# Maximum over the partitions: block transposes and small copies on VectorE instead of transposes on TensorE

## What is computed

```python
xn = _layernorm(x, axis=-1)
q = xn @ wq.T + bq;  k = xn @ wk.T + bk;  v = xn @ wv.T + bv
scores = jnp.einsum('bqd,bkd->bqk', q, k) * 256 ** -0.5
attn = softmax(scores, axis=-1) @ v
lilora = up_aux @ (lora_up @ (lora_down @ down_aux))
out = x + attn + (xn @ W.T + b) + xn @ lilora.T
```

## Time and profile before

| | |
|---|---|
| median of 3 runs | 580.87 us (580.44 to 581.39) |
| the profiled execution, its own time | 580.21 us |
| its span | 578.3 us |
| mean granted TensorE clock | 0.985 of full speed |
| TensorE busy (weight loads) | 549.9 us, 95% (518.6 us, 90%) |
| VectorE busy | 370.9 us, 64% |
| ScalarE busy | 308.9 us, 53% |
| GpSimd busy | 249.7 us, 43% |

### The profile page before, as it was taken

The page is one execution under the profiler, slowest core; times in us unless marked ns, Lnnn a source line. Parts: engine busy times, 40 slices in busy tenths (PEclk is TensorE's granted clock), DMA queues, the critical chain, the costliest instruction groups (busy, mean ns, idle before and its releaser), DMA issues.

```text
span 578.3 us, 10296 instructions
## 1 busy us (share of the span) xinstructions
PE 549.9 (95%) x3958; PEld 518.6 (90%) x3958; DVE 370.9 (64%) x873; ACT 308.9 (53%) x753; POOL 249.7 (43%) x149
## 2 busy tenths in 40 slices
PE   3898999999999999999999999999999999999995
PEld 2687999998999899999999989999999999999994
DVE  3555776666786576757766667866767576666671
ACT  3565346655565456573466655554565744544452
POOL 2801563454514663325634445146633256333333
PEclk9699899999999999999999999999999999999998
DMA  7100000011000300002000120002000000000001
GB/s 247 57 18 1 0 19 19 20 39 73 18 2 19 92 19 20 19 1 92 19 20 19 31 80 19 2 20 91 19 19 20 1 20 19 19 19 19 19 19 37
DMA packets 9300, 18.90 MB, mean 33 GB/s; under 512 B 2240, under 2 KB 3876, under 8 KB 8356
## 3 DMA queue, kind: packets, MB, share of 16 engines
q1 hardware_dynamic: 7712, 18.09, 9.0%
q10 hardware_dynamic: 1540, 0.16, 0.2%
HBM read 9.86 MB, written 8.39 MB: 32 GB/s over the span
## 4 chain that ended last, share of the span: by engine, by line
PE 79%; ACT 8%; DMA 6%; DVE 5%; issue 1%; POOL 1%; SPq 0%; ACTq 0%; POOLq 0%
PE s_ps L677 9%; PE s_ps L679 9%; PE o_ps L770 9%; PE s_ps L678 9%; PE o_ps L774 9%; PE o_ps L772 9%; PE g_ps L677 6%; PE g_ps L678 6%; PE g_ps L679 6%; DMA x_sb<-in_L_attn_x 5%; ACT s L426 4%; ACT p_hi L434 2%; PE g_ps L697 2%; PE g_ps L751 1%; DVE s L578 1%
## 5 line engine op out<-in xcount | busy, mean ns | idle before, releaser
L341 POOL TENSOR_TENSOR p_lo<-s,p_hi 128x1024 fp32r<-128x1024 f32 x64 | 153.8, 2404 | 307.1 <-ACT p_hi L434 196.8
L770 PE MATMUL o_ps<-v_hi,p_hi 128*128 128x258 f32 x512 | 149.8, 293 | 3.8 <-POOL p_lo L341 3.8
L677 PE MATMUL s_ps<-xt_hi,zt_hi 128*128 128x256 f32 x512 | 146.7, 287 | 0.0
L679 PE MATMUL s_ps<-xt_hi,zt_lo 128*128 128x256 f32 x512 | 145.4, 284 | 0.0
L678 PE MATMUL s_ps<-xt_lo,zt_hi 128*128 128x256 f32 x512 | 145.3, 284 | 0.0
L774 PE MATMUL o_ps<-v_hi,p_lo 128*128 128x258 f32 x512 | 144.8, 283 | 0.0
L772 PE MATMUL o_ps<-v_lo,p_hi 128*128 128x256 f32 x512 | 144.7, 283 | 0.0
L426 ACT ACTIVATE s<-s,e 128x256 f32<-128x256 f32 x256 | 109.3, 498 | 27.4 <-DVE s L578 27.4
L562 DVE SCALAR_TENSOR_TENSOR tile_max<-s_ps,e,tile_max 128x256 f32<-128x256 f32 x224 | 108.3, 484 | 23.4 <-PE s_ps L679 13.4
L770 PEld LDWEIGHTS o_ps<-v_hi,p_hi 128*128 128x128 f32 x512 | 96.9, 189 | 5.7 <-issue 3.9
L677 PEld LDWEIGHTS s_ps<-xt_hi,zt_hi 128*128 128x128 f32 x512 | 98.4, 192 | 1.9
(11 more groups left out here) (117 smaller groups left out, 739.4 us busy)
## 6 DMA issues: line engine op xcount, KB each, us to landing
out<-base SPq DMA_DIRECT2D x31, 256.0 KB, 2.5
x_sb<-in_L_attn_x SPq DMA_DIRECT2D x7, 1024.0 KB, 5.7
x_sb<-in_L_attn_x SPq DMA_DIRECT2D x4, 256.0 KB, 5.2
s<-in_L_attn_wk SPq DMA_DIRECT2D x1, 256.0 KB, 6.5
s<-in_L_attn_wq SPq DMA_DIRECT2D x1, 256.0 KB, 7.3
s<-in_L_attn_wv SPq DMA_DIRECT2D x1, 256.0 KB, 7.3
s<-in_L_ffn_W SPq DMA_DIRECT2D x1, 256.0 KB, 7.5
out<-base SPq DMA_DIRECT2D x2, 128.0 KB, 1.9
```

The source lines that it names most:

```text
L341: nc.gpsimd.tensor_tensor(p_lo[g % 2][:, keys, :], s[:, keys, :], p_hi[g % 2][:, keys, :].bitcast(f32), ALU.subtract)\
L677: nc.tensor.matmul(ps, left_hi(d), right_hi(d), start=(d == 0), stop=False)
L679: mm = nc.tensor.matmul(ps, left_lo(d), right_hi(d), start=False, stop=(d == DT - 1))
L770: nc.tensor.matmul(o_ps[u][:, 0:D + ONES], p_hi[g % 2][:, n, q], v_hi[i][:, n, :], start=(n == 0), stop=False)
```

## The change

The maximum over the partitions is made by VectorE alone, in a new `make_top`:

1. a 32x32 block transpose of `tile_max` into `tile_max_t` (each 32x32 block by itself): within each quadrant of 32 partitions the queries of a block now lie on the partitions;
2. a reduction over the 32 columns of each of the 8 blocks into `quad_max`, which leaves, in each of the four quadrants, the maxima over that quadrant's keys;
3. three copies that gather the other quadrants' results (32 x 8) beside those of the first;
4. a reduction over the four, into `max_col` (32 x 8);
5. three copies that spread it to the other quadrants;
6. a block transpose of `max_col` spread over 32 columns, into `top`.

All ten instructions are linked by semaphores where one needs the other. TensorE's `transpose_max` and `broadcast_max` are gone, and with them the waits of groups for the banks of the maximum; all groups now wait for the group two before them only. ScalarE's `make_top` is gone. In VectorE's loop the order changes too: `make_top`, `make_group_lo` of the second group and the four shifts come right behind the last `make_tile_max`, then `make_out`, then the statistics.

```diff
+            def make_top(g):
+
+                wait(dve, shifted, SB * g)
+                dve.wait_ge(tile_max_made, TILES * (g + 1))
+                nc.vector.transpose(tile_max_t[:, :], tile_max[:, :]).then_inc(max_t_made, 1)
+                dve.wait_ge(max_t_made, g + 1)
+                nc.vector.tensor_reduce(quad_max[:, 0, :], tile_max_t[:, :].rearrange("p (j k) -> p j k", k=BLOCK),
+                                        AXIS, ALU.max).then_inc(block_max_made, 1)
+                dve.wait_ge(block_max_made, g + 1)
+                for r in range(1, QUADS):
+                    nc.vector.tensor_copy(quad_max[0:BLOCK, r, :], quad_max[r * BLOCK:(r + 1) * BLOCK, 0, :])\
+                      .then_inc(quads_gathered, 1)
+                dve.wait_ge(quads_gathered, (QUADS - 1) * (g + 1))
+                nc.vector.tensor_reduce(max_col[0:BLOCK, :], quad_max[0:BLOCK, :, :].rearrange("p r j -> p j r"),
                                         AXIS, ALU.max).then_inc(max_col_made, 1)
+                dve.wait_ge(max_col_made, g + 1)
+                for r in range(1, QUADS):
+                    nc.vector.tensor_copy(max_col[r * BLOCK:(r + 1) * BLOCK, :], max_col[0:BLOCK, :])\
+                      .then_inc(quads_spread, 1)
+                dve.wait_ge(quads_spread, (QUADS - 1) * (g + 1))
+                nc.vector.transpose(top[:, :], max_col[:, :].unsqueeze(2).to_broadcast([PT, Q // BLOCK, BLOCK]))\
+                  .then_inc(top_made, 1)
...
@@ VectorE, start-up
-            make_group_lo(0, 2 * NT)
-            make_group_lo(0, 2 * NT + 1)
-            make_max_col(0)
-            make_group_lo(0, 2 * NT + 2)
-            make_group_lo(0, 2 * NT + 3)
+            make_top(0)
+            for n in range(4):
+                make_group_lo(0, 2 * NT + n)
...
@@ VectorE, loop
+                    if ahead:
+                        make_top(g + 1)
+                    if more:
+                        make_group_lo(b + 1, PLACES * c + 1)
+                    if ahead:
+                        for j in range(SB):
+                            shift(g + 1, j)
+                    make_out(b, c * QT)
                     if b + 2 < B and c < 3:
                         if c == 0:
                             dve.wait_ge(x_loaded[b % 2], DMA * ((b + 3) // 2))
                         make_stats(b + 2, [range(0, 2), range(2, 5), range(5, TILES)][c])
-                    if more:
-                        make_group_lo(b + 1, PLACES * c + 1)
-                    if ahead:
-                        make_max_col(g + 1)
                     if b + 2 < B and c == 2:
                         make_mean_var(b + 2)
-                    make_out(b, c * QT)
-                    if ahead:
-                        for j in range(SB):
-                            shift(g + 1, j)
...
@@ TensorE, a group's wait for its bank
-                if b > 0 and k % PLACES < 2:
+                if b > 0:
                     pe.wait_ge(group_done, max(NG * b + k - 1, NG))
-                elif b > 0 and k % PLACES == 2:
-                    pe.wait_ge(max_col_made, CHUNKS * (b - 1) + k // PLACES + 2)
-                elif b > 0:
-                    pe.wait_ge(top_made, CHUNKS * (b - 1) + k // PLACES + 2)
...
@@ TensorE, in p_times_v and the loop
-                    if u == 0 and n == TILES // 2 and ahead:
-                        transpose_max(g + 1)
...
-                        if u == 0 and ahead:
-                            broadcast_max(g + 1)
...
@@ ScalarE, loop
-                        make_top(g + 1)
```

More of the change, by code:

```diff
@@ L44, in attention_plus_lora_ffn @@
     ONES = 2
+    BLOCK = 32
+    QUADS = PT // BLOCK
     RANK, DDIM = lora_down.shape
@@ L120, in attention_plus_lora_ffn @@
         top = sb("top", [PT, Q])
-        max_col = sb("max_col", [PT, QT])
+        tile_max_t = sb("tile_max_t", [PT, Q])
+        quad_max = sb("quad_max", [PT, QUADS, Q // BLOCK])
+        max_col = sb("max_col", [PT, Q // BLOCK])
         s = sb("s", [PT, TILES, Q])
@@ L202, in attention_plus_lora_ffn @@
         tile_max_made = sem("tile_max_made")
-        max_t_mm = sem("max_t_mm")
+        max_t_made = sem("max_t_made")
+        block_max_made = sem("block_max_made")
+        quads_gathered = sem("quads_gathered")
         max_col_made = sem("max_col_made")
-        top_mm = sem("top_mm")
+        quads_spread = sem("quads_spread")
         top_made = sem("top_made")
@@ L240, in attention_plus_lora_ffn @@
         PLACES = NG // CHUNKS
[L242 to L246, removed]
         block = ctx.enter_context(nc.Block())
@@ L414, in make_e @@
                 nc.scalar.activation(e[b % 2][:, :], e_sum[:, :], ACT.Identity, bias=e_const).then_inc(e_made, 1)
[L416 to L420, removed]
             def make_p(g, j):
@@ L465, in _ @@
                 make_group_hi(0, 2 * NT + n)
-            make_top(0)
             for n in range(4, TILES):
@@ L555, in make_tile_max @@
                         dve.wait_ge(e_made, b + 1)
-                        wait(dve, max_t_mm, g)
+                        wait(dve, max_t_made, g)
                         nc.vector.tensor_scalar(tile_max[:, :], scores, e[b % 2][:, 0:1], None, ALU.add)\
@@ L563, in make_tile_max @@
                                                        ALU.add, ALU.max).then_inc(tile_max_made, 1)
[L565 to L569, removed]
-                                        AXIS, ALU.max).then_inc(max_col_made, 1)
+            def make_top(g):
[11 more added lines that the diff above has]
+                nc.vector.tensor_reduce(max_col[0:BLOCK, :], quad_max[0:BLOCK, :, :].rearrange("p r j -> p j r"),
+                                        AXIS, ALU.max).then_inc(max_col_made, 1)
+                dve.wait_ge(max_col_made, g + 1)
[5 more added lines that the diff above has]
+                  .then_inc(top_made, 1)
             def shift(g, j):
@@ L729, in scores, with p_times_v @@
                 mm.then_inc(score_mm, 1)
-            def transpose_max(g):
-                if g > 0 and (g - 1) // CHUNKS + 1 < B:
-                    pe.wait_ge(group_done, NG * ((g - 1) // CHUNKS + 1) + PLACES * ((g - 1) % CHUNKS) + 1)
-                else:
-                    wait(pe, max_col_made, g)
-                pe.wait_ge(tile_max_made, TILES * (g + 1))
-                for u in range(QT):
-                    mm = nc.tensor.transpose(max_bank(g)[:, u * PT:(u + 1) * PT], tile_max[:, u * PT:(u + 1) * PT],
-                                             identity[:, :])
-                mm.then_inc(max_t_mm, 1)
-            def broadcast_max(g):
-                if g > 0 and (g - 1) // CHUNKS + 1 < B:
-                    pe.wait_ge(group_done, NG * ((g - 1) // CHUNKS + 1) + PLACES * ((g - 1) % CHUNKS) + 2)
-                else:
-                    wait(pe, top_made, g)
-                pe.wait_ge(max_col_made, g + 1)
-                for u in range(QT):
-                    mm = nc.tensor.transpose(top_bank(g)[:, u * PT:(u + 1) * PT],
-                                             max_col[:, u:u + 1].to_broadcast([PT, PT]), identity[:, :])
-                mm.then_inc(top_mm, 1)
-            def p_times_v(g, u, ahead):
+            def p_times_v(g, u):
                 b, c = divmod(g, CHUNKS)
@@ L859, in _ @@
                     for u in range(QT):
-                        p_times_v(g, u, ahead)
-                        if u == 0 and ahead:
-                            broadcast_max(g + 1)
+                        p_times_v(g, u)
                         if more:
```

4 lines of the change are left out of this document (removed).

## The result

The changed kernel takes **561.19 us** (median of 4 runs, 560.42 to 561.81), beside 580.65 us for the kernel before on the same chip (4 runs, 579.35 to 581.39): a ratio of 0.967, with 95% from 0.9645 to 0.9688. Forecast were 560.0 us, in a range of 558.5 to 564.0. Its profiled execution took 560.91 us, with a span of 559.1 us (before 580.21 and 578.3) at a mean granted clock of 0.984 (before 0.985).

A forecast was written before the change was run, and what follows sets the result against it. TensorE was taken to bound the kernel (busy 66.25 of 67.50 us a batch). 12.9 + 7.4 + 0.5 + 0 = 20.8 us off 580.21 gives 559.4, so a median of 560.0 us, range 558.5 to 564.0.

The forecast's parts named there:

- The transposes: TensorE's stream: removing the transposes saves 0.43 us a block, over 30 blocks 12.9 us.
- The five waits: TensorE's waits ahead of L751 for max_col, behind statistics waiting for x: all go by the new order, 7.4 us.
- make_top: VectorE's new maximum over the partitions: 2.3 us, with 1.8 from below and 3.5 from above.
- twice three copies (0.08 + 0.08 + 0.19 = 0.35): In make_top on VectorE: each set of three small copies takes 0.35 us, 0.7 us for both sets.
- The ends: Kernel's two ends: last tile_max to first shift of block 31, 2.78 us before, gains 0.5 us; the start-up costs 0.
- The start: Start-up, tile_max to shifts on VectorE: make_top and four group_lo pairs fit, done at 47.7, cost 0.
- Room up to a top of 3.2: VectorE's spare time inside the batches: make_top may last up to 3.2 us at no cost there; 0.9 us to spare.
- A: Rival: make_top longer than 3.2 us but the scheme works; 565 us at 3.5, mostly 562 to 566; 12%.
- D: Rival: slower; make_top's ten steps cost 0.51 us each, 5.1 us, 584.4 us; slower than before from 4.8 us; 3%.
- B: Rival: the wait for x only moves and TensorE meets it at group 4; 7.4 us lost, 567.4 us; 7%.
- C: Rival: TensorE's transposes were hidden and removing them gives nothing; 572.9 us; 3%.
- copies would be held by 0.2 us: Block c = 0 of a batch: GpSimd's products hold VectorE's copies 0.2 us, taken in by the 0.9 us to spare.

The follow-up runs named there:

- transposes back: Changed kernel with two unused pairs of 128x128 transposes per block put back into TensorE's stream: 572.97 us, ratio 0.9868.
- statistics back: Changed kernel with the statistics of batch b+2 again ahead of make_top: 576.91 us, ratio 0.9935.
- p_hi first: Changed kernel with, in the last block, all products with p_hi made first and those with p_lo last: 556.67 us, ratio 0.9606.
- tile_max ahead: Changed kernel with tile_max of the first two banks ahead of the last group's lo part and of make_out: 561.73 us, ratio 0.9679.

## Why the prediction came out

The forecast was 1.2 us too low. Its two large terms were right and for the reasons given; two small ones were mis-sized, and the room it gave make_top was wrong in kind, which by luck didn't show.

1. **The transposes: right.** 12.9 us were put down; putting them back gave 11.8 between medians and 13.11 in the stretch.
2. **The five waits: right, and for the reason given.** 7.4 us were put down, the order alone gave 6.7 between medians and 7.53 in the stretch. Together the two terms are 20.3 us, and the stretch became 20.68 shorter.
3. **make_top: mis-sized.** Put at 2.3 us, it is 2.8 to 2.9. The large steps and the reduction were right (0.44 and 0.2 forecast, 0.445, 0.420 and 0.200 measured). Wrong was the step "twice three copies (0.08 + 0.08 + 0.19 = 0.35)": unlinked copies follow each other every 0.19, not 0.08, which makes 0.58 for each set and 0.46 of the difference. The row of bn_aggr was the wrong neighbour; the upper bound, "six copies one after another at 0.19", held. Nor was it so that none of the instructions is in the trace: the kernel before has a VectorE copy of 128x128 at L511 (224 ns) and the reduction of L569 (421 ns), both nearer than the rows taken. And the 311 ns that the prediction takes from the Trainium skill stand in VectorE: DVE Perf Modes under The three transpose paths, for 128x128 of bf16; the fp32 block transposes of 128x256 took 445 ns here.
4. **The ends: mis-sized by the same term.** The end was to gain 0.5. From tile_max to the first shift it was 2.78. After:

```profile
538.43 1.00 DVE L553 SCALAR_TENSOR_TENSOR tile_max<-s_ps,e,tile_max 128x256 f32<-128x256 f32 x2 [0.43 <-PE s_ps L684]
...
542.35 2.48 DVE L585 TENSOR_TENSOR s<-s_ps,top 128x512 f32<-128x512 f32 x4
```

   542.35 - 539.43 = 2.92: a loss of 0.14, and the last stretch as a whole is 0.30 longer. The start was put at 0. From tile_max (before 42.42, after 43.14) to the first shift (48.25, 49.43) it became 0.46 longer, again the copies. Another 0.72 us had passed before that tile_max ended, 0.4 of it in the wait for the load of wk (9.2 before, 9.6 after). One execution of each can't tell more: kernels with the same start-up reached the first group of batch 1 at 58.30 (transposes back), 59.52 (statistics back), 59.55 (p_hi first) and 61.33 us (tile_max ahead), so the 1.18 is one draw from a spread of 3 us. Together, 1.18 + 0.80 against forecast, less 0.4 from the stretch, are the 1.6 us by which the sum of 20.8 exceeds the difference of the spans, 19.2.
5. **The room: wrong, though it didn't decide.** "Room up to a top of 3.2" was read as the distance between one VectorE step and the TensorE step that needs it (0.9 forecast, 0.67 found). That bounds one late arrival. It says nothing of a ring in which each block's delay is handed to the next, and this had 0.16 us. Hence rivals A and D had slopes that were far too flat: at +0.58 us A's gave 3.8, measured were 13.5; D's point was at 4.8 us, and the runs put it near 3.6. A top of 3.2 us, which the forecast put at 562, would have come to some 565 to 568 (an estimate by the slope of 33 and the room of 0.16), above the range's end of 564. That the ring cost nothing was luck: the prediction never looked at it, and top fell 0.16 us short of its limit.
6. **The rivals.** B did not occur: with the statistics behind the shifts, x was in. C is refuted by the transposes put back. That copies would be held by 0.2 us was not needed for the sum: in the kernel after the longest copy of a set took 0.18. With GpSimd work through make_top, holding the copies costs nearly the entire gain (18.4 of 19.5 us).

## What to carry to other kernels

When work moves onto an engine with idle time, look for a cycle over that engine and its neighbours, and compare its length in one period with the bound engine's; the share of busy time and the distance to the next consumer don't show it, and a lengthening of the moved step by half a microsecond, in an experiment, does. Split a change that both reorders and replaces: here a third of the gain came from the order. And put small VectorE copies inside SBUF where GpSimd rests, or make them another operation: as reductions over one element they took 0.51 us in place of 2.44.

## What the runs showed of the hardware

- A VectorE copy inside SBUF (32x8) beside a running GpSimd product took up to 1.31 us in place of 0.16. A block transpose, a reduction and a copy written as a reduction over one element did not lengthen (0.45, 0.42, three in 0.51 us).
- The length of a wait alone doesn't tell whether TensorE's clock falls behind it. With the statistics back ahead of make_top, waits of 2.42 and 1.68 us were followed by granted clocks of 0.68 and 0.65, those of 1.93, 1.39 and 1.05 us by 1.00. Behind the 1.68 us and behind the 1.93 us:

```profile
340.90:344.00 3.10, 3.10 (x17) 2.92 (x18) 2.90 (x6) 2.52 (x6) 0.00 (x0) 0.65 0.00 0
```

```profile
273.76:278.00 4.24, 3.89 (x29) 3.51 (x30) 3.78 (x9) 3.66 (x9) 0.28 (x1) 1.00 0.01 4
```

- Unlinked copies of 32x8 last 0.16 us and start every 0.19; a copy of 64 times as many numbers (128x128, L511 before) lasts 0.22. At this size the amount moved hardly sets the price.
